# Half of the quantiser's clamp on ScalarE, layer 1's convolution lags placed earlier, and another end of the program

## The reference, cut to what matters

```python
# layer 0
x = x + attn0(gru(cond, x))        # GRU over 32 positions, one after the other; 16-head causal attention
x = x + ffn0(conv(x, cond) + b)    # convolution with per-sequence taps; int8 activations, ternary weights
# layer 1
x = x + attn1(cond_attn(x, cond))  # 16x16 heads with scale and shift; then rotary attention, 16 heads, one k and v
x = x + ffn1(conv(x, cond))        # y[t] = sum over lags 0..31 of tap[lag] * x[t - lag]; relu, square
# gru, one position
n = tanh(i_n + r * h_n);  h = (1 - z) * n + z * h
# ffn1's weights, before they are used: blocks of 64, 16 shrink factors s from 0.4 to 1.0
base = max|w| / 15
for s in SHRINKS:
    err[s] = sum((clip(round(w / (base * s)), -15, 15) * base * s - w) ** 2)
w = quantised with the s of the least err
```

## Time and profile before

| | |
|---|---|
| median of three runs | 1491.93 us (1489.49 to 1497.31) |
| the profiled execution | 1491.9 us, its span 1490.1 us |
| busy share of the span | TensorE 91%, VectorE 75%, ScalarE 55%, GpSimd 10% |
| instructions | 23006, of them 2862 on VectorE, 1694 on ScalarE |

### The profile page before, as it was taken

The page is one execution under the profiler, slowest core; times in us unless marked ns, Lnnn a source line. Parts: engine busy times, 40 slices in busy tenths (PEclk is TensorE's granted clock), DMA queues, the critical chain, the costliest instruction groups (busy, mean ns, idle before and its releaser), DMA issues.

```text
span 1490.1 us, 23006 instructions
## 1 busy us (share of the span) xinstructions
PE 1349.9 (91%) x7954; PEld 969.8 (65%) x7954; DVE 1119.1 (75%) x2862; ACT 824.9 (55%) x1694; POOL 146.7 (10%) x167
## 2 busy tenths in 40 slices
PE   6988888899999999999999967898999999999996
PEld 2433333578777777777877745475767777777765
DVE  4999999858857575757575979768687787878674
ACT  3866766875566666767676673534443434434221
POOL 0000000101010101010101100010210102020101
PEclk9999999989999999999999989798999999999999
DMA  9322333520111010101012310000000000000000
GB/s 379 97 64 64 71 84 81 153 79 29 36 36 43 29 43 29 43 29 43 29 44 82 149 64 8 22 15 1 15 12 10 14 7 21 7 8 8 8 8 15
DMA packets 26364, 73.78 MB, mean 50 GB/s; under 512 B 3977, under 2 KB 4885, under 8 KB 24993
## 3 DMA queue, kind: packets, MB, share of 16 engines
q1 hardware_dynamic: 25696, 71.62, 15.4%
q10 hardware_dynamic: 576, 0.98, 0.2%
HBM read 49.52 MB, written 23.07 MB: 49 GB/s over the span
## 4 chain that ended last, share of the span: by engine, by line
PE 52%; DVE 34%; ACT 7%; issue 5%; DMA 1%; SPq 1%; POOL 0%; DVEq 0%; ACTq 0%; POOLq 0%
PE psum L600 11%; PE psum L931 7%; PE psum L707 7%; DVE h_all L1820 5%; DVE work L1820 4%; PE psum L646 4%; PE psum L633 4%; DVE ffn_mem L1941 3%; PE psum L970 3%; DVE work L1952 3%; PE psum L960 2%; PE psum L613 2%; PE psum L877 2%; DVE work L1948 1%; ACT probs_t L1288 1%
## 5 line engine op out<-in xcount | busy, mean ns | idle before, releaser
L600 PE MATMUL psum<-h_all,w_big 128*128 128x256 f32 x1024 | 246.9, 389 | 3.9 <-ACT work L1246 3.9
L600 PEld LDWEIGHTS psum<-h_all,w_big 128*128 128x128 f32 x1024 | 190.3, 193 | 42.7 <-issue 13.5
L1820 DVE SCALAR_TENSOR_TENSOR work<-work,taps 128x248 f32<-128x248 f32 (+30 forms) x558 | 151.5, 346 | 0.0
L554 PE MATMUL psum<-w_big,h_all 128*64 128x512 f32 x512 | 124.1, 606 | 0.0
L931 PE MATMUL psum<-work,w_big 128*128 128x256 f32 x512 | 116.4, 380 | 0.0
L1820 DVE SCALAR_TENSOR_TENSOR h_all<-h_all,taps 128x248 f32<-128x248 f32 (+30 forms) x434 | 116.0, 342 | 0.0
L707 PE MATMUL psum<-w_big,gru_mem 128*128 128x256 f32 x512 | 113.6, 379 | 0.5 <-ACT gru_mem L1300 0.5
L707 PEld LDWEIGHTS psum<-w_big,gru_mem 128*128 128x128 f32 x512 | 96.4, 190 | 13.8 <-ACT gru_mem L1300 0.6
L931 PEld LDWEIGHTS psum<-work,w_big 128*128 128x128 f32 x512 | 95.5, 190 | 14.8 <-issue 2.5
L960 PE MATMUL psum<-w_big 128*128 128x256 f32 x448 | 105.0, 387 | 0.0
L1277 ACT ACTIVATE work<-psum 32x128 f32<-32x128 f32 x256 | 68.3, 267 | 53.7 <-PE psum L633 51.2
(11 more groups left out here) (316 smaller groups left out, 2628.1 us busy)
## 6 DMA issues: line engine op xcount, KB each, us to landing
value_rows<-w_emb SPq DMA_DIRECT2D x128, 128.0 KB, 2.3
work<-value_rows SPq DMA_DIRECT2D x16, 1024.0 KB, 5.8
w_big<-in_Wq SPq DMA_DIRECT2D x2, 2048.0 KB, 17.3
w_big<-in_Wo SPq DMA_DIRECT2D x2, 2048.0 KB, 21.8
out<-w_big SPq DMA_DIRECT2D x16, 256.0 KB, 2.0
x_res<-out SPq DMA_DIRECT2D x15, 256.0 KB, 2.7
w_big<-in_Wv SPq DMA_DIRECT2D x1, 2048.0 KB, 18.3
w_big<-in_Wk SPq DMA_DIRECT2D x1, 2048.0 KB, 23.8
```

Of the source, the lines that this page charges most:

```text
L554: mm = pe.matmul(bank(4 + n)[j * B:(j + 1) * B, :], h_all[:, k, :, 2 * pair + j], w_big[:, 2, k * H * HD + n * 512:k * H * HD + (n + 1) * ...
L600: mm = pe.matmul(bank(n % 2)[:, o * TA:(o + 1) * TA], w_big[:, s, k * H * HD + at:k * H * HD + at + HD], h_all[:, k, bass.ds(i * BA, BA), ...
L1820: ins = dve.scalar_tensor_tensor(dst[:, :, lag:], src[:, :, :T - lag], tap, dst[:, :, lag:], ALU.mult, ALU.add)
```

## The change

Five edits.

1. `round_off` clamps only the lower half of a group (`HALF = 2` factors, 896 elements). The upper half is done by ScalarE: `from_top` makes relu(MAGIC + 15 - v), that is 15 minus the clamped number. VectorE's rest then has the other sign of the scale and carries +15, which the second of two half-size Squares takes off with a bias column of -15.
2. The GRU's bias is split into three parts in place. Each part is subtracted only in the rows that hold a later part (the table `bias_pick` is now a lower triangle with a minus), with five operations in place of eight on the rows. With the copy of `bias_pick` that stays, six stand where nine did.
3. In `chunk1` lags 4 to 6 stand ahead of `rot_soft_in`. `cond_rms`' two reductions are run through `clink`, so a head operation is drawn behind each of them. Two semaphores (`css_on`, `s1_on`) fall into `c_step` and `r_step`.
4. At the end `keep_x3` stands ahead of the first relus, ScalarE squares its relus itself in the last two chunks (`own_squares`), and lags 7 to 31 have a new line that only the trip without `cond` reads.
5. The last chunk is multiplied into two banks, added and stored in two halves.

```diff
+HALF = 2
+        shr_top = tally("shr_top", NG)
+        def pj_out(c, g):
+            return bank(6 + g)[:, 0:D] if isinstance(c, int) and c == NA - 1 else bank(6)[:, g * D:(g + 1) * D]
+        def own_squares(c):
+            return isinstance(c, int) and c >= NA - 2
...
+            for g in range(GA):
+                sp.wait_ge(y_on.sem, NA + g)
+                sp.dma_start(out[:, GA * (NA - 1) + g:GA * (NA - 1) + g + 1, :], y_buf[:, g:g + 1, :]).then_inc(y_out, 16)
...
+            def from_top(n):
+                upper = w5_tmp[n % NG][:, HALF:GROUP, :]
+                act.wait_ge(shr_raised.sem, n + 1)
+                act.activation(upper, upper, ACT.Relu, bias=top_col[:], scale=-1.0).then_inc(shr_top.sem, 1)
+
             def squares(n):
                 act.wait_ge(rest_on.sem, n + 1)
-                act.activation(w5_tmp[n % NG], w5_tmp[n % NG], ACT.Square).then_inc(sq_on.sem, 1)
+                lower, upper = w5_tmp[n % NG][:, 0:HALF, :], w5_tmp[n % NG][:, HALF:GROUP, :]
+                act.activation(lower, lower, ACT.Square)
+                act.activation(upper, upper, ACT.Square, bias=less_col[:]).then_inc(sq_on.sem, 1)
...
                 if t >= 2:
                     squares(t - 2)
+                from_top(t)
...
                     act.activation(relu[:, f % 2, :], bank(f % 2)[:, 0:TA], ACT.Relu).then_inc(relu_on.sem, 1)
+                    if own_squares(c):
+                        act.wait_ge(relu_on.sem, KF * c + f + 1)
+                        act.activation(h2_t[:, f, :], relu[:, f % 2, :], ACT.Square).then_inc(h2_on.sem, 1)
...
+                if rot and not cond:
+                    keep_x3(i)
                 if ffn:
                     relus(ni, range(0, 2))
                 if prep:
                     row_squares(i + 2)
-                if rot and not cond:
-                    keep_x3(i)
...
             dve.wait_ge(bias_in, 16 * 2)
-            for j in range(3):
-                link(dve.tensor_copy(bias_parts[j], bias_f))
-                if j < 2:
-                    link(dve.tensor_tensor(bias_f, bias_f, bias_parts[j], ALU.subtract))
             bias_on.raised_by(dve.tensor_copy(bias_pick, pick_f[:, 0:P]))
-            link(dve.tensor_scalar(bias_rows, bias_parts[0], pick_f[:, P:P + 1], None, ALU.mult))
...
+            for j in range(2):
+                link(dve.tensor_copy(bias_rows, bias_f))
+                link(dve.scalar_tensor_tensor(bias_f, bias_rows, pick_f[:, P + 1 + j:P + 2 + j], bias_f, ALU.mult, ALU.add))
+            bias_on.raised_by(dve.tensor_copy(bias_rows, bias_f))
...
-                dve.tensor_scalar(w5_tmp[g], w5_tmp[g], MAGIC + QMAX, MAGIC, ALU.min, ALU.subtract).then_inc(shr_cut.sem, 1)
+                lower = w5_tmp[g][:, 0:HALF, :]
+                dve.tensor_scalar(lower, lower, MAGIC + QMAX, MAGIC, ALU.min, ALU.subtract).then_inc(shr_cut.sem, 1)
                 dve.wait_ge(shr_cut.sem, n + 1)
+                dve.wait_ge(shr_top.sem, n + 1)
...
+                    ins = dve.scalar_tensor_tensor(tmp, w5_abs[q % 2], -scale if j < HALF else scale, tmp,
...
+                    clink(dve.tensor_reduce(c_ms[:, 32 * g:32 * g + 32],
+                                            c_sq[:, g, :].rearrange("p (e d) -> p e d", d=CD), AX.X, ALU.add))
...
                 turn_heads(H)
+                conv2(range(4, 7))
                 if rot:
                     rot_soft_in(i, 0, rlink)
...
                 if begun:
                     add_ffn(e, 1)
+                if rot and not cond:
+                    conv2(range(7, T))
...
-                conv2(range(4, 10))
+                if cond:
+                    conv2(range(7, 10))
                 if cond:
                     cond_soft_out(ci, 1, clink)
...
+                        for g in range(GA):
+                            dve.wait_ge(pj_sum.sem, ni + g + 1)
+                            dve.tensor_tensor(y_buf[:, g, :], pj_out(ni, g), ffn1(ni)[0][:, g, :],
```

More of the change, by code:

```diff
@@ L98, in layers @@
         magic_col = sb("magic_col", [P, 1])
+        top_col = sb("top_col", [P, 1])
+        less_col = sb("less_col", [P, 1])
         h_all = sb("h_all", [P, KD, B, T])
@@ L156, in layers @@
         bias_f, bias_rows, bias_pick = start_rows[:, 0:4 * P], start_rows[:, 512:768].bitcast(BF16), start_rows[:, 768:832].bitcast(BF16)
-        bias_parts = [work[0:12, 4608 + 256 * j:4864 + 256 * j].bitcast(BF16) for j in range(3)]
         pick_f = stats[0:12, 0:P + 3]
@@ L516, in _ @@
                     load_r(c + 2)
-                store(c)
-            sp.wait_ge(y_out, (NA + 1) * 16)
+                if c < NA - 1:
+                    store(c)
+            for g in range(GA):
+                sp.wait_ge(y_on.sem, NA + g)
+                sp.dma_start(out[:, GA * (NA - 1) + g:GA * (NA - 1) + g + 1, :], y_buf[:, g:g + 1, :]).then_inc(y_out, 16)
+            sp.wait_ge(y_out, (NA + 2) * 16)
         @block.tensor
@@ L994, in pj @@
                     for f in range(KF):
-                        mm = pe.matmul(bank(6)[:, g * D:(g + 1) * D], h2_t[:, f, g * P:(g + 1) * P], proj_t[:, f, :],
+                        mm = pe.matmul(pj_out(c, g), h2_t[:, f, g * P:(g + 1) * P], proj_t[:, f, :],
                                        start=(f == 0), stop=(f == KF - 1))
-                if GA - 1 in groups:
+                    if isinstance(c, int) and c == NA - 1:
+                        mm.then_inc(pj_sum.sem, 1)
+                if GA - 1 in groups and not (isinstance(c, int) and c == NA - 1):
                     mm.then_inc(pj_sum.sem, 1)
@@ L1746, in relu_squares @@
             def relu_squares(c, tiles):
-                for f in tiles:
+                for f in (() if own_squares(c) else tiles):
                     pool.wait_ge(relu_on.sem, KF * c + f + 1)
@@ L2450, in chunk1 @@
                     cond_soft_in(ci, 1, clink)
-                conv2(range(4, 10))
+                if cond:
+                    conv2(range(7, 10))
                 if cond:
                     cond_soft_out(ci, 1, clink)
-                conv2(range(10, T))
+                if cond:
+                    conv2(range(10, T))
                 if cond:
@@ L2464, in chunk1 @@
                     dve.wait_ge(y_out, 16 * ni + 16)
-                    dve.wait_ge(pj_sum.sem, ni + 1)
-                    dve.tensor_tensor(y_buf.rearrange("p g n -> p (g n)"), bank(6),
-                                      ffn1(ni)[0].rearrange("p g n -> p (g n)"), ALU.add).then_inc(y_on.sem, 1)
+                    if rot:
+                        dve.wait_ge(pj_sum.sem, ni + 1)
+                        dve.tensor_tensor(y_buf.rearrange("p g n -> p (g n)"), bank(6),
+                                          ffn1(ni)[0].rearrange("p g n -> p (g n)"), ALU.add).then_inc(y_on.sem, 1)
+                    else:
+                        for g in range(GA):
+                            dve.wait_ge(pj_sum.sem, ni + g + 1)
+                            dve.tensor_tensor(y_buf[:, g, :], pj_out(ni, g), ffn1(ni)[0][:, g, :],
+                                              ALU.add).then_inc(y_on.sem, 1)
                 if rot and cond:
```

29 lines of the change are left out of this document (12 added, 17 removed).

## The result

The changed kernel takes 1473.96 us (median of four runs, 1473.78 to 1474.45), the kernel before 1491.16 us in the same comparison (1489.49 to 1497.31). The ratio is 0.9874, with a 95% interval from 0.9857 to 0.9891: 17.2 us faster where 14.6 were forecast, and inside the range.

The account below looks back on a forecast made before the run. The bound changes with the stage: VectorE in the steps, TensorE then VectorE in a layer 1 iteration, both in turn at the end. 1491.9 - 11.3 (steps) - 0.6 (layer 1) - 2.7 (end) = 1477.3 us, range 1470 to 1486.

Parts of the forecast that it names:

- The clamp: Recurrent steps: halving VectorE's clamp gains 0.47 us in each of 26 steps, -12.2 us; +1.3 early, -0.4 at stage's end.
- The bias part: Step 0: nine small VectorE operations become six, worth nothing, since VectorE waits there for the constants' load.
- (A): Rival in the steps: ScalarE leads them, with the Relu ahead of the gates, so slower, total 1515 us; 3%.
- (B): Rival: the steps give nothing, their stage's end set by something the clamp doesn't move, 1488.6 us; 9%.
- (C): Rival in layer 1: the moved lags pay in full, 12.6 in place of 0.6, 1465.3 us; 4%.
- (D): Rival in layer 1: head operations cost nothing (1475) or 0.9 us each (1481.5), inside the range; no chance given.
- Layer 1's body: Layer 1's iterations: moved lags -2.7 us and head operations ahead of the normalisation +2.1 us, together -0.6 us.
- The delay at the transposes: Layer 1: two head operations ahead of L2300 make TensorE's transposes L893 wait 0.3 us, +2.1 us over seven iterations.
- the lags' gain: Layer 1: moving lags 4 to 6 gains 0.55 us in five iterations, -2.7 us, limited by ScalarE's exponential.
- Bounds: 0 if the gaps close, 0.9 if nothing hides it: Layer 1: limits in us on the 0.3 us wait at TensorE's transposes L893 caused by the two head operations.
- The end: Program's end: earlier `keep_x3` -2.0 us, ScalarE squaring the last relus -0.4, halved last add and store -0.3; sum -2.7.
- (b): Program's end: ScalarE squares the last relus itself, 0.85 us in place of GpSimd's 1.22, -0.4 us.

Follow-up runs that it names:

- the run with three quarters: The changed kernel with HALF = 1, so that ScalarE clamps three of the four factors instead of half: 1473.39 us.
- the three with the earlier exponential: Changed kernel, ScalarE's second condition exponential ahead of its rotary-output copies: 1464.67 us; also without head operations behind the reductions: 1461.85 us (HALF = 1), 1460.67 us (HALF = 2).

## Why the prediction was right, point by point

**The bound of each stage** was read rightly: VectorE in the steps, with ScalarE and TensorE close behind.

**The clamp.** Forecast -12.2 over 26 steps, +1.3 early, -0.4 at the tail. Measured from step 5's tanh to step 31's: 11.14 + 1.35 = 12.5 in 26 steps, 0.48 each; early +1.35. The tail gave nothing: ScalarE's wait for the `w_down` load ends 10.93 us earlier (284.36 in the earlier trace rows against 273.43), 0.2 less than the last tanh's lead, not 0.4 more. At the stage's end 10.9 for 11.3.

**The rule against it.** The Trainium skill, ScalarE: Activation LUTs, section Rules for kernel authors, puts relu, max and min on VectorE and so speaks against the edit. On price the trace agrees, 1.12 us of ScalarE's time a step for 0.48 of VectorE's; on the step it does not hold here, because ScalarE had room. The run with three quarters shows where it begins to: once ScalarE leads, more of the clamp there gains nothing.

**The bias part**: nothing, as forecast. **The rivals**: (A) did not come, and the run with three quarters shows its mechanism; (B) falls with the steps' 11.1 us; (C) falls with the 0.38 to 0.70 an iteration, and the exponential that it needed earlier gives it when it is put there; (D) came at its middle, with the later pauses on top.

**Layer 1's body.** Forecast -0.6, measured +2.85 between the first and the sixth product. The change itself is 0.3 of that: 69.03 us for 68.93 in four iterations and, at full clock, 68.72 (the kernel with three quarters) for 68.83 in the fifth. The delay at the transposes is the forecast 0.3, the lags' gain 0.70 in the changed kernel where 0.55 was forecast, and what failed is the term "Bounds: 0 if the gaps close, 0.9 if nothing hides it", which counted the head operations at the transposes alone; another 0.2 to 0.5 came behind them. The rest, 2.55 us, is the granted clock: three of the five products ran into the low level in the changed kernel, one of the same five before.

**Between the steps and layer 1** the forecast had nothing, and the lead grew by 2.6 us. One piece of it, in layer 0, before and then changed:

```profile
380.00:388.00 8.00, 7.70 (x35) 5.49 (x36) 6.62 (x19) 5.22 (x9) 0.70 (x1) 0.79 0.10 33
```

```profile
368.90:376.90 8.00, 7.70 (x46) 5.33 (x47) 6.62 (x19) 6.04 (x11) 0.70 (x1) 1.00 0.10 34
```

The same stretch of the same work, after pauses of 2.81 and 2.83 us of TensorE, was granted 0.79 in one execution and 1.00 in the other, and VectorE's lead grows by 1.4 us across it (the convolutions of layer 0 start 11.10 us earlier in the changed kernel ahead of it and 12.47 behind it). Another piece lies at 958 us of before: the same sixteen products (L960, now L973) take 5.46 us there, begun at the low level, and 3.72 in the changed kernel. No moved instruction is in either. But whether the other level is chance or comes with the changed timing is not shown: there is one trace of each kernel, and the changed kernel's four runs lie within 0.7 us of each other. Over all runs but the three with the earlier exponential the distance from step 31's tanh to the first product is 777.5 to 781.1 us, and the changed kernel has the 777.5.

**The end.** Forecast -2.7, measured -7.2: 2.0 of `keep_x3` (forecast 2.0), 2.2 of the convolution that GpSimd no longer slows (not forecast), 1.7 of the sixth product's clock (8.86 us before, 7.17 changed), 0.5 of the last product (9.38 and 8.86, both begun at the low level; the forecast took none), 0.2 of the squares (forecast 0.4), 0.6 of the half-size add and store (forecast 0.3). The step that failed is (b): it priced the squares on ScalarE by their own lengths alone and did not ask what GpSimd's squares did to VectorE's convolution beside them, though the trace of before had the answer, 18.59 us here and 16.38 in layer 0, with six lags nearly twice as long as the same lags there.

So the mechanisms of the steps and of `keep_x3` were right to a few tenths. Without the missed 2.2 us of the convolution and the clock's 2.2 (2.6 between the stages and 2.2 at the end for the changed kernel, 2.55 in the iterations against it) the lead would be 13.7 us, 0.9 under the forecast. That the clock's parts came to no more than 2.2 us in sum is luck: they could have added up.

## What to carry to other kernels

Before work is moved between engines, look at what it slows beside it: the same lags with two durations in one trace (0.81 to 0.86 and 0.45 to 0.47 us) are the sign. A whole group is a weaker sign, since other work can stand between its parts: layer 0's convolutions take from 16.38 to 20.95 us. Idle time before a wait is room only above what stays idle when that engine itself sets the pace, and a filled pause gives back only what the next wait lets through: here that wait was an exponential behind copies, and putting it first was worth 1.59 us an iteration. Where differences are a few microseconds, compare iteration with iteration at the same granted clock, not totals.
